# Dense query pieces prepared inside the main block, and mask flags loaded one score pair sooner

## The reference, cut to what matters

```python
q = hidden_state @ Wq + bq                # 32 x 56 x 256
k = encoder_hidden_state @ Wk + bk        # 32 x 1500 x 64
v = encoder_hidden_state @ Wv + bv
scores = jnp.einsum('bkgld,bksd->bkgls', q, k) * scale
scores = scores + encoder_attention_mask[:, :, None, :, :]
attn = jax.nn.softmax(scores, axis=-1)
out = jnp.einsum('bkgls,bksd->bkgld', attn, v)
x = out.reshape(b, l, H) @ Wo + bo + hidden_state     # then a layer norm
```

## Time and profile before

| what | before |
|---|---|
| median of 3 runs | 3539.97 us |
| range of the runs | 3537.3 to 3543.28 us |
| the profiled execution, its own time | 3543.89 us |
| its span, first to last instruction | 3542.1 us |
| TensorE busy (matmul) | 2912.3 us, 82% |
| VectorE, ScalarE, GpSimd busy | 58%, 40%, 18% |
| mean granted TensorE clock | 0.912 |

### The profile page before, as it was taken

The page is one execution under the profiler, slowest core; times in us unless marked ns, Lnnn a source line. Parts: engine busy times, 40 slices in busy tenths (PEclk is TensorE's granted clock), DMA queues, the critical chain, the costliest instruction groups (busy, mean ns, idle before and its releaser), DMA issues. The chain is left out here.

```text
span 3542.1 us, 64209 instructions
## 1 busy us (share of the span) xinstructions
PE 2912.3 (82%) x18753; PEld 1523.6 (43%) x18753; DVE 2040.3 (58%) x4206; ACT 1411.9 (40%) x3023; POOL 652.5 (18%) x487
## 2 busy tenths in 40 slices
PE   4699999999999998998657757699999979766775
PEld 2244444444444444443323323366666546333332
DVE  7467677767767676774546546244444420546644
ACT  3155555555555555555121111244444432121121
POOL 6211222221222221220312212000000000312321
PEclk8699999999999999999878878799999989878887
DMA  7434433433443433430100000111111100100000
GB/s 208 114 104 120 120 111 115 113 92 110 120 120 106 120 101 94 120 102 16 58 0 0 0 0 0 51 32 31 31 31 31 25 27 0 55 0 0 0 0 21
DMA packets 114573, 221.46 MB, mean 63 GB/s; under 512 B 12545, under 2 KB 78830, under 8 KB 113902
## 3 DMA queue, kind: packets, MB, share of 16 engines
q1 hardware_dynamic: 114286, 217.58, 22.0%
HBM read 167.11 MB, written 50.09 MB: 61 GB/s over the span
## 5 line engine op out<-in xcount | busy, mean ns | idle before, releaser
L589 DVE CUSTOM_DVE_ANT_0 masked<-ps_a,mask 112x750 f32<-112x750 f32 x1024 | 941.8, 936 | 396.8 <-PE ps_a L476 383.6
L549 ACT ACTIVATE probs<-ps_a 128x448 f32<-128x448 f32 (+1 forms) x1536 | 742.6, 542 | 549.7 <-PE ps_a L442 546.4
L476 PE MATMUL ps_a<-ks,q_row 96*112 96x375 bf16 x2048 | 530.3, 342 | 56.5 <-DVE part_max L589 33.1
L442 PE MATMUL ps_a<-q_sc,ks 99*128 99x448 bf16 (+1 forms) x1536 | 453.2, 360 | 50.6 <-ACT probs L549 30.3
L462 PE MATMUL ps_a<-probs,vp 128*32 128x224 f32 x6144 | 378.1, 364 | 1.3 <-ACT probs L549 0.9
L476 PEld LDWEIGHTS ps_a<-ks,q_row 96*112 96x112 bf16 x2048 | 221.9, 133 | 325.3 <-issue 263.7
L1858 DVE CUSTOM_DVE_ANT_0 f_masked<-ps_c,f_mp 112x432 f32<-112x432 f32 x256 | 145.5, 605 | 222.7 <-PE ps_c L1710 220.3
L442 PEld LDWEIGHTS ps_a<-q_sc,ks 99*128 99x128 bf16 (+1 forms) x1536 | 132.8, 100 | 282.2 <-issue 232.3
L226 POOL CAST k_piece<-kv_t 64x1500 bf16<-64x1500 f32 x32 | 45.7, 1428 | 1056.4 <-ACT kv_t L218 1056.4
L205 PE MATMUL ps_a<-ctx_t,wkv 128*128 128x375 f32 x512 | 197.0, 510 | 42.1 <-PEq L266 24.9
L462 PEld LDWEIGHTS ps_a<-probs,vp 128*32 128x32 f32 x6144 | 163.0, 110 | 159.1 <-issue 58.3
(11 more groups left out here) (287 smaller groups left out, 3984.2 us busy)
## 6 DMA issues: line engine op xcount, KB each, us to landing
ctx_t<-in_ctx_t SPq DMA_DIRECT2D x32, 1500.0 KB, 10.3
ks<-k_scr SPq DMA_DIRECT2D x64, 562.5 KB, 5.1
mask<-in_mask SPq DMA_DIRECT2D x64, 328.1 KB, 5.8
k_scr<-k_piece SPq DMA_DIRECT2D x32, 562.5 KB, 8.3
k_scr<-k_piece SPq DMA_DIRECT2D x32, 375.0 KB, 8.3
f_context<-in_ctx_t SPq DMA_DIRECT2D x32, 375.0 KB, 3.2
q_row<-q_scr SPq DMA_DIRECT2D x32, 336.0 KB, 5.7
q_sc<-q_scr SPq DMA_DIRECT2D x32, 336.0 KB, 6.5
```

What stands on the lines that cost most here:

```text
L442: mm = pe.matmul(out, ks[par][:, j, at], q_sc[par][:, j], start=True, stop=not with_mask)
L476: mm = pe.matmul(ps[0:2 * L, bank + i, 0:SC], q_row[which][:, j, h, gp * 2 * L:(gp + 1) * 2 * L], ks[which][0:SROWS, j, at], start=True, s ...
L549: act.activation(probs[t % 2][0:n, i], ps[0:n, k % SCORE_BANKS, 0:PW] .rearrange("p (h n) -> p h n", h=2), ACT.Exp).then_inc(probs_done, 1)
L589: dve.tensor_tensor_reduce(out=masked[:, u % 2], in0=two_banks(bank, 2 * L), in1=in_two(mask[which][:, c * SU:(c + 1) * SU]), scale=1.0, s ...
```

## The change

It has five parts.

1. The query pieces are stored without zeros. q_scr and k_scr keep the two halves of the 64 channels apart, a query load is two transfers of 84 KB (384 pieces of 448 bytes in all), each into its half of the 96 rows and its half of the columns, and the zeros stand in the four query tiles from the start (six memsets on GpSimd, two of them the rows of ones of ks that VectorE set before). Rounding is one operation per piece. Key stores are six in place of three, with the same bytes; the slots of a piece are taken with a step (slots_of).
2. There are two piece buffers and one residue tile in place of three and two; a chunk is stored in six transfers with half the bytes.
3. The early stage's work stands at the head of the main block, with no barrier between. SP issues batch 0's loads after chunk 0's stores, and batch -1's after the last chunk's.
4. x_nat's bias comes after the last chunk on VectorE, and TensorE waits for it before its first body.
5. TensorE's last pair of scores of step 11 and the front work behind it go from the end of body b - 1 to the head of body b, behind the loads of the flags: the one of batch b - 1 again, and that of batch b.

The diff, cut to its core:

```diff
-K_PIECES = (0, 0, 0, 1, 1, 2)
-Q_PIECES = (0, 1, 2, 0, 1, 0)
+K_PIECES = (0, 0, 0, 1, 2, 1)
+Q_PIECES = (2, 1, 0, 0, 0, 1)
+def slots_of(pieces, r):
+
+    slots = [i for i in range(NS) if pieces[i] == r]
+    step = slots[1] - slots[0] if len(slots) > 1 else 1
+    return slice(slots[0], slots[-1] + 1, step), len(slots)
...
+    q_scr = nc.dram_tensor("q_scr", [2, NS, KVH * HD // 2, B, QW], BF16).ap()
+    k_scr = nc.dram_tensor("k_scr", [2, 2, NS, KVH * HD // 2, S], BF16).ap()
...
         def load_q(sp, b, to, which):
 
-            sp.dma_start(to, q_view[bass.ds(b, 1)].rearrange("o p j h n -> p (o j) h n")).then_inc(which, 16)
+            for h in range(2):
+                sp.dma_start(to[h * SROWS // 2:(h + 1) * SROWS // 2, :, h],
+                             q_view[h, bass.ds(b, 1)].rearrange("o p j n -> p (o j) n")).then_inc(which, 16)
...
+        def store_q(sp, c):
+
+            sp.wait_ge(q_lo, c + 1)
+            for r in range(3):
+                at, count = slots_of(Q_PIECES, r)
+                for h, on in HEADS:
+                    sp.dma_start(q_scr[h, at, :, c * CH:(c + 1) * CH].rearrange("s d b n -> d s (b n)"),
+                                 qp[c % 2][on, r:r + 1].to_broadcast([KVH * HD // 2, count, CH * QW]))\
+                      .then_inc(q_out[c % 2], 16)
...
+            store_k(sp, 0)
+            store_q(sp, 0)
+            sp.wait_ge(q_out[0], 16 * Q_STORES)
+            sp.wait_ge(zeroed, ZEROS)
+
+        def early_pool(pool):
+
+            zeros = [(tile[:], 0.0) for tile in q_row + q_sc] + [(tile[SROWS:MROWS], 1.0) for tile in ks]
+            for n, (where, value) in enumerate(zeros):
+                pool.memset(where, value).then_inc(zeroed, 1)
+                pool.wait_ge(zeroed, n + 1)
+            split_k(pool, 0, kv_t[0][0:KVH * HD])
+            for c in range(CHUNKS):
+                pool.wait_ge(q_mid, c + 1)
+                pool.tensor_tensor(qp[c % 2][:, 2], flat(qr[:]), qp[c % 2][:, 1], ALU.subtract).then_inc(q_lo, 1)
+
+        def early_pe(pe):
...
+            pe.wait_ge(q_add, G * CHUNKS)
+            pe.wait_ge(kv_read, NKV)
+            pe.wait_ge(preset, ONES)
+            pe.wait_ge(zeroed, ZEROS)
+            pe.wait_ge(x_bias, 2)
+
+        def early_dve(dve):
...
+                dve.wait_ge(q_hi, c + 1)
+                if c >= 1:
+                    dve.wait_ge(q_lo, c)
+                dve.tensor_tensor(flat(qr[:]), flat(q32[c % 2][:]), qp[c % 2][:, 0], ALU.subtract).then_inc(q_r1, 1)
+            dve.wait_ge(late_loaded, 16 * LATE_LOADS)
...
+        def early_act(act):
...
+            for c in range(CHUNKS):
+                act.wait_ge(q_add, G * (c + 1))
+                if c >= 2:
+                    act.wait_ge(q_out[c % 2], 16 * Q_STORES * (c // 2))
+                act.activation(qp[c % 2][:, 0], flat(q32[c % 2][:]), ACT.Copy).then_inc(q_hi, 1)
+                act.wait_ge(q_r1, c + 1)
+                act.activation(qp[c % 2][:, 1], flat(qr[:]), ACT.Copy).then_inc(q_mid, 1)
...
             cur, prev = there("row", b), there("row", b - 1)
+            flag_of = {}
+            if prev:
+                flag_of[nx] = pe.value_load(flag[0:1, nx:nx + 1], min_val=0, max_val=1)
             if cur:
                 wait_apart(pe, passed, flag_done, b + 1)
-                masked_cur = pe.value_load(flag[0:1, par:par + 1], min_val=0, max_val=1)
-
-            def scores(t, pair):
+                flag_of[par] = pe.value_load(flag[0:1, par:par + 1], min_val=0, max_val=1)
+
+            def scores(b, par, t, pair):
...
-                with pe.If(masked_cur):
+                with pe.If(flag_of[par]):
...
+            if prev:
+                scores(b - 1, nx, NT - 1, 1)
+            if not known or b > -2:
+                front(b - 1, nx, NT - 1, 2)
             for t in range(NT):
                 if cur:
-                    scores(t, 0)
-                front(t, 0)
+                    scores(b, par, t, 0)
+                front(b, par, t, 0)
...
-                front(t, 1)
-                if cur:
-                    scores(t, 1)
-                front(t, 2)
+                front(b, par, t, 1)
+                if t < NT - 1:
+                    if cur:
+                        scores(b, par, t, 1)
+                    front(b, par, t, 2)
...
             @block.sync
             def _(sp):
-                all_bodies(sp, sp_body)
+                early_sp(sp)
+                sp_body(sp, -2, 0)
+                for c in range(1, CHUNKS):
+                    store_q(sp, c)
+                for i in range(2):
+                    sp.wait_ge(q_out[i], 16 * Q_STORES * len(range(i, CHUNKS, 2)))
+                all_bodies(sp, sp_body, -1)
```

More of the change, by code:

```diff
@@ new lines, in layer0 @@
+        CHUNKS = B // CH
+        LATE_LOADS = 6
+        x_t = sb("x_t", [P, KC, T])
+        q32 = [sb(f"q32_{i}", [KVH * HD, CH, QW]) for i in range(2)]
+        qr = sb("qr", [KVH * HD, CH, QW])
+        qp = [sb(f"qp{i}", [KVH * HD, 3, CH * QW], BF16) for i in range(2)]
+        loaded, preset, q_mm, q_add, q_hi, q_r1 = map(sem, "a_loaded a_preset q_mm q_add q_hi q_r1".split())
+        q_mid, q_lo, x_bias, kv_loaded, zeroed, late_loaded = map(
+            sem, "q_mid q_lo x_bias kv_loaded zeroed late_loaded".split())
@@ new lines, in early_dve @@
+        def early_dve(dve):
+            sets = [(ones[:], 1.0)]
+            for i in range(2):
+                sets += [(vp[i][:], 0.0), (vp[i][:, :, :, HD:HD + 1], 1.0)]
+            for n, (where, value) in enumerate(sets):
+                dve.memset(where, value).then_inc(preset, 1)
+                dve.wait_ge(preset, n + 1)
+            dve.wait_ge(loaded, 48)
+            for c in range(CHUNKS):
+                for g in range(G):
+                    dve.wait_ge(q_mm, G * c + g + 1)
+                    if c >= 2:
+                        dve.wait_ge(q_hi, c - 1)
+                        dve.wait_ge(q_r1, c - 1)
+                    dve.tensor_scalar(q32[c % 2][:, :, g * L:(g + 1) * L],
+                                      ps[0:KVH * HD, Q_BANKS[g], 0:CW].rearrange("p (b l) -> p b l", l=L),
+                                      bq[:, g:g + 1], float(HD) ** -0.5, ALU.add, ALU.mult).then_inc(q_add, 1)
+                dve.wait_ge(q_hi, c + 1)
+                if c >= 1:
+                    dve.wait_ge(q_lo, c)
+                dve.tensor_tensor(flat(qr[:]), flat(q32[c % 2][:]), qp[c % 2][:, 0], ALU.subtract).then_inc(q_r1, 1)
+            dve.wait_ge(late_loaded, 16 * LATE_LOADS)
+            dve.tensor_copy(identb[:], ident[:]).then_inc(x_bias, 1)
+            dve.tensor_tensor(x_nat[:], x_nat[:], bo[:].unsqueeze(1).to_broadcast([P, PAIRS, E]),
+                              ALU.add).then_inc(x_bias, 1)
+            dve.wait_ge(x_bias, 2)
@@ L398, in sp_body @@
                 load_mask(sp, b + 1, nx, 1)
-                load_q(sp, b + 1, q_sc[nx][0:SROWS].rearrange("p j (h n) -> p j h n", h=2), qs_in)
+                load_q(sp, b + 1, q_sc[nx][:].rearrange("p j (h n) -> p j h n", h=2), qs_in)
             if there("kv", b + 3) and (not known or b > -2):
@@ L487, in turn_v, with front @@
                 mm.then_inc(vt_mm, 1)
-            def front(t, place):
+            def front(b, par, t, place):
+                nx = 1 - par
                 for at, (step, pos, kind, off, i) in enumerate(FRONT_UNITS):
@@ L658, in pool_body, with all_bodies @@
                 split_k(pool, b + 3, kv_t[nx][0:KVH * HD])
-        def all_bodies(eng, body):
-            for b in range(-2, 1):
+        def all_bodies(eng, body, first=-2):
+            for b in range(first, 1):
                 body(eng, b, b % 2)
```

182 lines of the change are left out of this document (51 added, 131 removed).

## The result

The changed kernel takes **3530.55 us** (median of 14 runs, 3527.78 to 3538.49), the kernel before in the same comparison 3541.38 (14 runs, 3535.68 to 3545.9): a ratio of 0.9973, 95% interval 0.9965 to 0.9981, some 10 us (0.3%) faster. The forecast was 3537.0, its range 3514 to 3563. The profiled execution took 3530.8 us, with a span of 3528.7. Of all runs in this text one, a run of e9 at 4649 us, fell in a slow state and is left out of its median.

A forecast was written before the change was run, and what follows sets the result against it. TensorE was taken to bound the main loop, but not the early stage. Early stage -21, query loads -6, flags +20 gave -7; +4 for clock falls made -3, so 3537 us, range 3514 to 3563.

The forecast's parts named there:

- The forecast's own signs: First projection near 79.5 us, boundary idle rows of about 0.9 and 0.55, no ctx_t wait, half-clock stretches behind laps or more.
- Early stage, forecast -21: Before the main stage: halved rounding work and later bias let TensorE start near 79.5 us against 100.35, gaining 21 us.
- the turn of a buffer: Early stage: with two piece buffers, stores two chunks back set the pace, 11.6 us for two chunks, 5.8 a chunk.
- Query loads, forecast -6: Main loop: smaller query loads let ctx_t land 0.7 us sooner, removing nearly all TensorE waits for it, some 6 us.
- the step that took the removed wait as a gain of the same size: Loop, step 3: removing TensorE's 4.6 us of ctx_t waits in 21 batches gains 4.6 x 28/21, some 6 us.
- Time goes with bytes: Query loads ahead of ctx_t: if bytes set transfer time, ctx_t lands 0.7 us sooner; if by packet, not at all.
- The rival of small packets: Query loads: 448 B pieces slower than 896 B ones, each batch waiting 1.2 us more; 3575 us, chance 0.05.
- Flags, forecast +20: Batch boundaries: moved flag loads and last pair cost a net +0.65 us at each of 31 boundaries, +20 us.
- +4 for the clock: TensorE: one or two further falls of its clock add 4 us to the sum.
- the step of +0.65 us per boundary: Boundary: losses of 1.0 ahead of the last pair and 0.85 before the next scores, less 1.2 us of old loss.
- the rival "clock": Loop: two idle gaps also drop TensorE's clock at ordinary boundaries, +10 to +30 us, 3547 to 3567; chance 0.27.
- Everything after layer 0 is untouched: Layers behind layer 0: the change does not touch them, so no term was given for them.

The follow-up runs named there:

- e9: e1 plus 36 TensorE instructions in layer 1 that only wait for a semaphore already reached: 3503.45 us, ratio 0.9887 to the kernel before.
- e4: e1 with three query piece buffers in place of two: 3503.96 us, ratio 0.9896 to the kernel before.
- e5: e4 with x_nat's bias put after the sums of chunk 2 instead of behind the last chunk: 3496.49 us, ratio 0.9874 to the kernel before.
- e1: The changed kernel without its flag part (one load at the head, last pair back in step 11): 3508.40 us, ratio 0.9902 to the kernel before.
- e6: e1 with the loads of q_sc doubled, the second copy into a tile nobody reads: 3519.51 us, ratio 0.9935 to the kernel before.
- e0: The changed kernel again, unedited, as the base for the others: 3528.11 us, ratio 0.9957 to the kernel before.
- e2: The kernel before with the flag part of the change alone: 3565.44 us, ratio 1.0065 to the kernel before.
- e10: e8 plus the same 36 waiting TensorE instructions without effect as in e9: 3478.60 us, ratio 0.9814 to the kernel before.
- e8: e5 with TensorE's waits for the next batch moved ahead of the last pair of step 11: 3479.46 us, ratio 0.9831 to the kernel before.
- e7: The kernel before with a second, unused load of the flag at the head of the body: 3571.23 us, ratio 1.0071 to the kernel before.

## Why the prediction was right, and where not

The median came out 10.8 us below before, for -3 forecast; 3530.55 lies in the range, 6.5 below the point. The forecast's own signs held: an early stage far under 90 us, two idle rows, almost no wait for ctx_t, a few stretches at half clock besides the laps'.

- **Early stage, forecast -21, measured -25.7.** The mechanism held to the row: one operation of 64x896 for two of 32x896, the split of k done at 27.9 us (27.7 said), pieces waiting for the stores of the chunk two before, the bias last. The mis-sized term is the turn of a buffer, "11.6 us for two chunks"; it is 9.7. From the end of a low piece (53.44) to the next high piece in that buffer (58.14) it is 4.7 us, where six issues and a landing were put at 6.3; the stores took 0.48 to issue and 2.6 to land at the median. The four operations took 5.0 for 5.3. e4 shows that the buffers were the limit, and e5 that most of an earlier start reaches the end.
- **Query loads, forecast -6, some -8 measured, but not where it was put.** e1 against before is free of the flags. Its layer 0 is 33.8 us shorter, and all but 25.7 of that lies behind the start. Up to batch 24 it is only 1.6. TensorE's waits for ctx_t fell from 4.6 us to nothing there, as forecast, but its idle time before row products (waits for VectorE's part_max, and for its own queue) rose from 31.0 to 35.6. So the step that took the removed wait as a gain of the same size failed in the loop, and that the total is near is luck. Of the other 6.5 us 2.3 are waits for ctx_t behind batch 24, and 1.3 is a stall of VectorE behind the last lap, 4.8 us of TensorE's time before and 3.5 in e1, which no step foresaw; there TensorE also stood at half clock for 6.8 us and not 10.2. "Time goes with bytes" is what the ctx_t rows and e6 show. The rival of small packets fell. The Trainium skill, "DMA: Bandwidth & Descriptors", Specifications, says that transfers below 512 B are done by read-modify-write. This case shows no such price: with 39681 packets below that size on the page after, against 12545 before, the ctx_t transfer behind the query loads landed sooner.
- **Flags, forecast +20 and +4 for the clock; measured +20 (median, e0 against e1) and +22.5 (e2), but 26 to 32 in layer 0.** The medians agree because the layers behind became shorter at the same time. In layer 0 the changed kernel is 26.3 us (e0) and 31.5 us (the profiled execution) above e1. Measured from step 11 to step 11, an ordinary batch of the loop grew from 46.88 us (e1) to 47.24, so the step of +0.65 us per boundary is 0.36: the two losses came out 0.76 and 0.42 us of idle, not 0.9 and 0.55. A lap's first batch grew by 1.9 us, from 50.5 to 52.4: mostly 10.2 us at half clock and not 6.8. Each extra fall behind an ordinary boundary costs 2.9 (50.1 against 47.24); the profiled execution had three and e0 one. 18 x 0.36 + 6 x 1.9 + 3 to 9 is 21 to 27 up to batch 24, as the table shows (21.1 and 26.4); some 5 us more lie behind it. Up to batch 24 the changed kernel was at half clock for 22 us (e0) to 35 us (profiled) more than e1, which at half speed costs 11 to 17. So the clock's part was put at 4 and is 11 to 17, and the idleness was put at 20 and is some 15. The mechanism of the rival "clock" happened, above all at the laps' ends that were long already, and at one to three of the ordinary boundaries. With 7 to 13 us over the forecast it reached just the lower end of that rival's price (+10 to +30), and it did not decide, since the other terms came out better.
- **Layers behind, forecast 0, measured -8 to -11 in the profiles.** "Everything after layer 0 is untouched" was the step that failed. The work is untouched, but the place of its instructions is not. e9 and e10 show that instructions without effect take the stall of 3 us away. Of the 11.1 us between before and the changed kernel TensorE's idle time is 5.7 and its busy time on the same matmuls 5.4; how the part beside the stall hangs on it is not shown. The Trainium skill, "Runtime: NRT & Kernel Launch", Instruction fetch mechanics, says that instructions come in blocks of 256 and that a taken branch can break the fetch ahead. Two rows go with it: the stall stands near the end of layer 2's loop and cuts a group of like products, and 36 instructions ahead of it are enough to remove it. That it is the fetch is argued and not measured.

In the profiled execution the parts add up: -25.7 - 8.1 + 31.5 - 11.1 = -13.4 us, the difference of the spans. Layer 0 itself came out at -2.3 (e0: -7.5) for the -3 that the sum gave. That this is so close is luck: the early stage, the loads and the idleness each came out 2 to 6 us better than forecast, and the clock 7 to 13 worse. The median's distance from the forecast is about the size of the term that was put at nothing.

## What to carry to other kernels

Read the sequencer's own rows at a batch's boundary before moving an instruction that reads a register: ahead of a full queue it is free, but two of them drained a lead of 1 us and made a second gap, while moving three already satisfied waits into the slack ahead of the boundary gained 17 us from e5 to e8. Price a new gap by what it does to the clock of the next microseconds too, which here was about half of the cost. And where a difference of a few microseconds decides, test the parts from both sides (one undone, one alone) and look at the stages that were not touched.

## What the runs showed of the hardware

- A gap of 1.84 us, two pairs of products and a gap of 0.53 us were followed by 10.2 us at 1.2 GHz; one of 1.84 alone (e1) by 6.8; one of 1.4 (e8) only once in the loop. 0.76 and 0.42 (changed) or 1.62 (e7) brought it on at some ordinary boundaries and not at others. The length of the gap alone does not decide: one lap's end with 1.82 us (e6) and one with 2.49 us (e7) were followed by no stretch at half clock. Their rows, of e6 and then of e7:

```profile
575.71 0.60 PE L448 MATMUL ps_a<-q_sc,ks 99*128 99x448 bf16 x2 [1.82 <-issue]
```

```profile
608.55 0.68 PE L443 MATMUL ps_a<-q_sc,ks 99*128 99x448 bf16 x2 [2.49 <-issue]
```

- The ctx_t transfer landed 13.2 us after a batch's first scores with 336 KB of queries ahead of it, whether these were 384 packets of 896 B (before) or 768 of 448 B (e6), and at 12.4 to 12.6 with 168 KB in 384 packets of 448 B (changed, e1).
- A load of one register costs TensorE's queue some 0.65 us (0.3 of it the load itself), and a branch 0.45 or more, of which its row shows 0.21. "Releaser ACT probs" was named on gaps that ended with a branch.
- Kernels that differ only in instructions without effect differed by 7.0 us (e1 and e9) and 9.7 us (e8 and e10) in the layers that follow, of which 3 are a stall of TensorE that one has and the other has not; two executions of one kernel differed there by 3.3.
